# Six extra TensorE matmuls ahead of every group in the three row-gather sums of a graph network

## What is computed

```python
def _spmm(vals, rows, cols, x, n):
    gathered = vals[:, None] * x[cols]
    return jax.ops.segment_sum(gathered, rows, num_segments=n)
# third layer: side = _spmm(edge_weight, src, dst, x, n); (x + 3 * side) / 4
# fourth layer, only its last of three rounds counts:
ht = jnp.einsum('ne,reh->rnh', hidden, weights[l])
msg_f = ht[edge_type, src] + biases[l][edge_type]
out = jax.ops.segment_sum(msg_f, dst, num_segments=n_nodes)
msg_b = ht[edge_type + n_rel, dst] + biases[l][edge_type + n_rel]
out = out + jax.ops.segment_sum(msg_b, src, num_segments=n_nodes)
```

## Time and profile before

| | us |
|---|---|
| median of 3 runs | 8027.81 |
| lowest and highest | 8021.37, 8035.16 |
| the profiled execution | 8034.51 |
| its span | 8032.7 |
| mean granted TensorE clock | 0.652 |

### The profile page before, as it was taken

One profiled execution on the slowest core, in us unless ns is written; L12 is line 12 of the kernel. 1 busy time (PEld: TensorE's weight loads), 2 busy tenths in 40 slices (PEclk: granted clock), 3 DMA queues, 4 the chain that ended last, 5 costly groups with the idle time before them and its releaser, 6 DMA issues. The chain is left out here.

```text
span 8032.7 us, 65229 instructions
## 1 busy us (share of the span) xinstructions
PE 2904.5 (36%) x12802; PEld 2351.3 (29%) x12803; DVE 2420.6 (30%) x4511; ACT 334.4 (4%) x878; POOL 4435.6 (55%) x5226
## 2 busy tenths in 40 slices
PE   0023333336644444442663333326333333233332
PEld 0012222235522222222552222223222222222222
DVE  2630000037734444445774122214111110011111
ACT  0001111100000000001001000000000000000000
POOL 0027777742226666662444666761666666776665
PEclk9985555567767777776885555557565555555555
DMA  2113223234426666664441111113211111111111
GB/s 87 26 57 95 85 90 93 88 83 116 105 78 170 172 172 170 171 169 115 122 121 33 47 44 47 46 45 148 66 45 45 45 45 43 47 46 45 45 45 46
DMA packets 688109, 674.55 MB, mean 84 GB/s; under 512 B 216326, under 2 KB 550142, under 8 KB 684346
## 3 DMA queue, kind: packets, MB, share of 16 engines
q0 software_dynamic: 144176, 323.21, 13.8%
q1 hardware_dynamic: 377036, 256.76, 11.6%
q10 hardware_dynamic: 166848, 94.11, 4.1%
HBM read 524.45 MB, written 164.31 MB: 86 GB/s over the span
## 5 line engine op out<-in xcount | busy, mean ns | idle before, releaser
L763 PE MATMUL ps<-g_got,g_hot 128*128 128x128 f32 x4896 | 1100.5, 383 | 2458.9 <-issue 1369.6
L763 PEld LDWEIGHTS ps<-g_got,g_hot 128*128 128x128 f32 x4896 | 986.1, 289 | 2573.5 <-issue 2572.8
L731 POOL DMA_INDIRECT g_got<-y,d_msg x816 | 820.2, 1005 | 526.4 <-issue 246.0
L731 POOL DMA_INDIRECT g_got<-x,s_dst x816 | 804.9, 986 | 443.3 <-issue 243.0
L731 POOL DMA_INDIRECT g_got<-y,s_msg x816 | 815.2, 999 | 369.3 <-issue 247.4
L562 POOL DMA_INDIRECT msg<-sr_pay,sr_place x816 | 801.8, 983 | 323.2 <-issue 290.7
L1077 POOL DMA_INDIRECT sc_kv<-kv,sc_cur x816 | 786.6, 964 | 264.9 <-issue 256.5
L742 DVE TENSOR_TENSOR g_hot<-col,src_loc 128x1024 f32<-128x1024 f32 x204 | 247.5, 1224 | 1922.5 <-remote 1100.4
L515 PE MATMUL ps<-x_rows,sr_hotT 128*128 x1632 | 382.7, 360 | 803.7 <-issue 745.1
L515 PEld LDWEIGHTS ps<-x_rows,sr_hotT 128*128 128x128 f32 x1632 | 319.2, 261 | 865.9 <-issue 864.6
L1165 PE MATMUL ps<-q,sc_hotT 128*128 x1632 | 299.3, 341 | 557.1 <-issue 401.2
(11 more groups left out here) (238 smaller groups left out, 2975.4 us busy)
## 6 DMA issues: line engine op xcount, KB each, us to landing
sr_locb<-loc SPq DMA_DIRECT2D x204, 256.0 KB
sc_locb<-loc SPq DMA_DIRECT2D x204, 256.0 KB
ve<-sc_kve ACTq DMA_DIRECT2D x204, 256.0 KB
wv_ve<-ve SPq DMA_DIRECT2D x102, 512.0 KB, 3.9
y<-ms_y SPq DMA_DIRECT2D x25, 1152.0 KB, 4.2
fs_got<-msg ACTq DMA_DIRECT2D x408, 66.5 KB, 1.9
fs_got<-msg SPq DMA_DIRECT2D x408, 66.5 KB, 1.9
msg<-sr_pay,sr_place POOLq DMA_INDIRECT x816
```

Of the source, the lines that this page charges most:

```text
L731: pool.indirect_dma_start(out=got[:, q, j, :], out_offset=None, in_=table, in_offset=bass.IndirectOffsetOnAxis(ap=index[:, c:c + 1], axis= ...
L763: last = pe.matmul(ps[:, bass.ds(columns[j], width)], hot[:, q, j, :], got[:, q, j, 0:width], start=False, stop=True, skip_group_check=True)
```

## The change

A helper makes `count` matmuls of the identity (stationary) and the first 512 columns of `x` (moving) into the eighth bank of `ps`, which the sums do not use. In `gather_sum` TensorE calls it with 6 for every group, after the column numbers are loaded and ahead of the two waits. Nothing reads the bank. The number of waits and semaphore counts is the same as before.

```diff
+def keep_running(pe, S, count):
+
+
+    for _ in range(count):
+        pe.matmul(S["ps"][:, 7 * BANK:8 * BANK], S["ident"][:, :], S["x"][:, 0:BANK], start=True, stop=True)
+
+
@@
             with pe.Fori(0, WHOLE) as i:
                 for q in range(WAYS):
                     columns = load_columns(nc, S, mybir.EngineType.PE, name, 1, start_of(i, q))
+                    keep_running(pe, S, 6)
                     pe.wait_ge(heated[q], i + 1)
                     pe.wait_ge(landed[q], (i + 1) * (16 * GROUP))
                     for j in range(GROUP):
```

## The result

The changed kernel takes **8147.16 us** (median of 4 runs, 8133.70 to 8162.59) against 8024.85 for the kernel before (4 runs, 8021.37 to 8035.16): ratio 1.0151, 95% interval [1.0129, 1.0173], so 122 us slower. The profiled execution reads 8153.8 us with a span of 8151.8, where the one before had 8032.7.

The account below looks back on a forecast made before the run. It took GpSimd's gathers to set the sums' pace, at 10.0 us per group, plus waits for TensorE. 8034.5 us plus 34 + 34 + 70 + 80 = +218, less 4.5, gave 8250 us; range 7690 to 8650.

Parts of the forecast that it names:

- the likeliest case: Whole kernel: slower at 8250 us, 2.8%, with its own range 8080 to 8500 us and a chance of 50%.
- slow stretches: In the three sums: times when TensorE's single passes come 2.1 to 3.5 us apart, about 46 us long in the last two.
- The clock near 0.8: TensorE in the three sums: mean clock would rise from 0.56 of full to near 0.8.
- The price of a group: TensorE's time per group with added passes: 7.8 us at the high clock, 13.8 us at the low one.
- More waits after the slow stretches: GpSimd's waits for TensorE: 13.4 instead of 11 in each of the last two sums, +34 us each; first sum +70.
- The last term: After a release, the awaited group runs behind added passes: 4 to 7 us in half of some 45 waits, +80 us.
- The end of each sum: Last group of each sum: real matmuls 1.5 us shorter, so 3 x 1.5 = 4.5 us gained.
- slower gathers, most of them right behind such a wait: GpSimd's gathers in the sums before the change: 117 us of excess, 1.42 us instead of 0.94 behind a wait.
- The mask on VectorE has the same slack as the gathers: VectorE's masks in the sums: five groups or 50 us of slack.
- The two readings on the stretches: In the sums: TensorE's idling does not bring a stretch on, and a stretch ends soon after GpSimd stops.
- Rival (b), everything is covered: In the sums: added passes take only idle time and TensorE catches up as before, 8030 us; chance 15%.

Follow-up runs that it names:

- e5_after_again: The changed kernel itself, unaltered, run again in a later group of runs: ratio 1.0138 to the kernel before.
- e1_narrow: The changed kernel with its six added matmuls cut from 512 columns to 16: ratio 0.9999 to the kernel before.

## Why the prediction came out as it did

The sign, the range and the likeliest case held: 2.8% slower was forecast, 1.5% measured. That the number is this near is in good part luck, for its terms did not come true. The forecast put all of its 218 us on waits that grow behind the slow stretches, nothing on the masks and a small gain on the ends of the sums. The 119 us between the two spans are 24 of waits, some 32 of gathers held up by masks and 63 at the ends. Step by step:

- **The clock near 0.8**: right, 0.80 in all three sums. The price of a group was near: 6.93 us at the high clock (5.15 of added passes and 1.78 of real ones) where I had 7.8. The prediction ends by saying that at 6.5 us the loss would halve, and the measured loss is about half, but this is no proof of that working, since the term it speaks of brought 24 us.
- **More waits after the slow stretches**: right in direction, wrong in size and shape. I had 13.4 waits in each of the last two sums, about as long as before. There were 26 in each, mostly 4 to 6 us long, three or four groups apart instead of nine. In time they cost little: 380 us against 338. By the records of TensorE's single passes, g3 had 11 stretches of 46 us with 59 us between them; in the changed kernel it has 27 of 19 us with 25 us between. The step that failed is that the 56 us from a release to the next stretch, and nearly the whole length of a stretch, stay as they are: all stretches of g3 together last some 510 us in both traces, cut into more and shorter pieces. The last term was too low even by its own figures, 4 to 7 us in half of 45 waits being 90 to 158 us and not 80.
- **The end of each sum, "3 x 1.5 = 4.5 us" gained**: wrong in sign. It assumed that TensorE is one group behind at the last gather. With slow stretches it is several behind there, even where the last stretch ended 20 us earlier (g4), and each then costs 6.9 us instead of some 2: +63 us, half the loss. It is the slow catching up that the prediction describes, at a place where the prediction counted a gain. In the runs without stretches this term is zero.
- **The "slower gathers, most of them right behind such a wait"**: misread, and it hid the next step. In the trace of before the gathers are 129 us longer than 0.944 us each, and only 48 us of this is in the two gathers behind a wait of over 1.5 us. Of the 262 gathers that took over 0.03 us more than usual, 260 started while a mask was running.
- **"The mask on VectorE has the same slack as the gathers"**: the step that left something out. The mask's result has slack, but its start does not leave GpSimd alone. I read the 1.42 us gather of the earlier trace rows as something a wait leaves behind. It is a mask: the same release sets off VectorE and GpSimd together, as the timeline of the kernel before shows, where three masks in a row end at 6060.02 and the gather of 6058.87 ends at 6060.83, again 0.81 us later.

```profile
6056.52 3.50 DVE L742 TENSOR_TENSOR g_hot<-col,dst_loc 128x1024 f32<-128x1024 f32 x3 [24.76 <-remote]
6057.15 1.42 POOL L731 DMA_INDIRECT g_got<-y,d_msg  x1 [9.58 <-remote]
6058.87 1.96 POOL L731 DMA_INDIRECT g_got<-y,d_msg  x1 [0.30 <-issue]
```

- **The two readings on the stretches**: that TensorE's idling doesn't bring them fits, since with the clock at 0.80 they came more often, not less; that they end soon after GpSimd stops fits too, for they became shorter as its buffers ran out sooner. Both rest on the first pair of traces alone. What brings the stretches on stays open: none of the experiments' runs had them. That the masks explain the 33 us of longer gathers in that pair is read from its traces, not tried. There the cost by phase is the same (median 0.19 us at 0.3, 0.77 at 0.9, 0.94 at 1.1 in the trace of before), and the gathers that start in a mask are 154 us longer than usual in the changed kernel where they were 123 us longer before, 31 of the 33 us.
- **Rival (b), everything is covered**: its condition was met in all the experiments' runs, where no slow stretch builds a backlog, and it would have said no change. They gave 1.38% slower. So there the prediction would have had the sign right for a wrong reason: its waits are not there at all, and the masks are the whole loss.

## What to carry to other kernels

An engine that is far off the critical path can still set the pace of another by when it starts, so before shifting the timing of one engine, look at who starts while who is running; gathers whose durations fall in two heaps (0.94, and 1.1 to 2 us) are the sign. Where GpSimd issues DMAs back to back, cutting VectorE's long comparisons into short ones is worth a try: here it gave 0.4% with four parts and 0.9% with eight. Other instructions of VectorE were not tried. A faster clock is worth only the time of what the end waits for: here 0.66 and 0.81 ran in the same time once the masks were out of the way. And work that is added to fill idle time must not stand between a backlog and its catching up.

## What the runs showed of the hardware

- A comparison of 128x1024 fp32 with both operands in SBUF (1.22 us) holds up the start of an indirect DMA on GpSimd until its end; the gather ends 0.81 to 0.82 us later. A gather that has already started isn't held up. A running gather doesn't hold up a mask: in e5_after_again masks that start 0.1 to 1.1 us after a gather's start take 1.225 to 1.227 us. Only a mask within some 0.05 us of a gather's start is held, to 1.30 us at most.
- The Trainium skill, "SBUF — State Buffer", section "SBUF: two separate sides", says that VectorE and GpSimd share a pair of ports under an exclusive lock, that an instruction of VectorE with two SBUF inputs takes part in it, though only against a GpSimd instruction that reads SBUF, and that whichever starts first has the pair for its whole instruction. The gather takes its row numbers from SBUF, and that it waits for the mask's end agrees. That the lock lasts for GpSimd's whole instruction does not show: a mask begun 0.3 us into a gather of 0.94 us ran at its usual length. No run here shows that the ports are the reason, nor which part of the gather needs them.
- The slow stretches, in which TensorE's items come singly, were in both traces of the first pair, and in no other. The send stage had its in that pair too. The kernel before took 8025 us with them and 7250 us without. Set against e1_narrow, which runs like the kernel before, 412 us of the difference lie ahead of the first sum and 375 between the first and the last gathers of the three sums. VectorE is slow in a stretch too: its mask for the group whose passes ended at 5991.52 starts at 6030.54, after 42 us in which it waited for nothing that the profile shows. An optimisation aimed at the stretches would have found nothing in the second case.

```profile
6030.54 1.22 DVE L742 TENSOR_TENSOR g_hot<-col,dst_loc 128x1024 f32<-128x1024 f32 x1 [42.18 <-issue]
```
